# Another order in the first two steps of a Mamba mixer: third projection pair before the cumulation, softplus in two parts

## The reference

```python
h = rmsnorm(layernorm(x), ln1_w)
z, xs, Bs, Cs, dt = split(h @ w_in.T)               # widths 512, 128, 128, 512, 4
xs, Bs, Cs = silu(conv4(concat(xs, Bs, Cs)) + conv_b) # causal, depthwise, 4 taps
dt = softplus(dt + dt_bias)
a = dt * -exp(A_log)
cs = cumsum(a, within each chunk of 128)
att = (Cs @ Bs.T) * exp(cs_q - cs_k)[lower triangle] * dt_k
y = att @ xs + (Cs @ state) * exp(cs) + D * xs      # state carried from chunk 0 to chunk 1
out = (y * silu(z)) @ w_out.T
```

## Time and profile before

| What | Value |
|---|---|
| median of 3 runs | 1748.95 us (1748.63 to 1749.5) |
| profiled execution, its own time | 1752.33 us |
| its span | 1750.6 us |
| PE busy | 1644.1 us, 94% |
| DVE busy | 1084.1 us, 62% |
| ACT busy | 792.1 us, 45% |
| POOL busy | 604.3 us, 35% |
| mean granted clock of PE | 0.986 of full speed |

### The profile page before, as it was taken

The page is one execution under the profiler, slowest core; times in us unless marked ns, Lnnn a source line. Parts: engine busy times, 40 slices in busy tenths (PEclk is TensorE's granted clock), DMA queues, the critical chain, the costliest instruction groups (busy, mean ns, idle before and its releaser), DMA issues. The chain is left out here.

```text
span 1750.6 us, 26151 instructions
## 1 busy us (share of the span) xinstructions
PE 1644.1 (94%) x8965; PEld 1378.9 (79%) x8965; DVE 1084.1 (62%) x2298; ACT 792.1 (45%) x1723; POOL 604.3 (35%) x792
## 2 busy tenths in 40 slices
PE   4999999999999999999999999988999999999984
PEld 4898987888888888777877888767888888888873
DVE  6888876525565554574334233556777877877773
ACT  3676664223223232222222222217877777776860
POOL 4455463211111111432111111465354444444422
PEclk8999999999999999999999999999999999999997
DMA  4000011000111101421011011210000000000000
GB/s 138 21 17 21 1 37 53 25 25 22 30 28 42 35 17 35 130 71 57 16 34 38 28 37 48 73 37 13 1 7 7 13 1 14 13 1 13 14 7 19
DMA packets 32967, 54.26 MB, mean 31 GB/s; under 512 B 3840, under 2 KB 9120, under 8 KB 32832
## 3 DMA queue, kind: packets, MB, share of 16 engines
q1 hardware_dynamic: 32832, 52.55, 9.8%
HBM read 43.10 MB, written 9.44 MB: 30 GB/s over the span
## 5 line engine op out<-in xcount | busy, mean ns | idle before, releaser
L1280 POOL TENSOR_TENSOR m_a_lo<-m_prod,m_a_hi 128x512 fp32r<-128x512 f32 x100 | 134.8, 1348 | 635.4 <-ACT m_a_hi L1362 635.4
L1515 DVE TENSOR_TENSOR m_prod<-m_prod,a_ps 128x512 f32<-128x512 f32 x100 | 68.8, 688 | 386.4 <-ACT m_prod L1356 386.4
L1356 ACT ACTIVATE m_prod<-a_ps 128x512 f32<-128x512 f32 x100 | 59.8, 598 | 546.3 <-PE a_ps L128 546.3
L2074 ACT ACTIVATE t_p<-a_ps,t_nmax 128x128 f32<-128x128 f32 (+1 forms) x512 | 182.9, 440 | 4.7 <-DVE t_nmax L2171 3.8
L2177 DVE TENSOR_TENSOR t_pT_lo<-a_ps,t_pT_hi 128x512 fp32r<-128x512 f32 x192 | 132.5, 690 | 73.5 <-ACT t_pT_hi L2067 72.6
L2171 DVE TENSOR_REDUCE t_nmax<-a_ps 128x2 f32<-128x512 f32 (+1 forms) x192 | 131.1, 683 | 24.9 <-PE a_ps L2249 18.1
L2067 ACT ACTIVATE t_pT_hi<-a_ps 128x512 fp32r<-128x512 f32 x192 | 118.6, 618 | 61.4 <-PE a_ps L2260 60.6
L128 PE MATMUL a_ps<-m_hT_hi,m_w_lo 128*128 128x512 f32 x312 | 123.9, 397 | 0.0
L126 PE MATMUL a_ps<-m_hT_hi,m_w_hi 128*128 128x512 f32 x312 | 123.1, 395 | 0.4 <-DVE f_w_lo L1420 0.4
L127 PE MATMUL a_ps<-m_hT_lo,m_w_hi 128*128 128x512 f32 x312 | 123.3, 395 | 0.0
L2260 PE MATMUL a_ps<-consts,t_p 128*128 128x128 f32 x768 | 115.8, 273 | 0.8 <-ACT t_p L2074 0.6
(11 more groups left out here) (287 smaller groups left out, 4677.6 us busy)
## 6 DMA issues: line engine op xcount, KB each, us to landing
m_raw<-in_w_mlp SPq DMA_DIRECT2D x75, 256.0 KB, 2.7
a_xt<-in_x SPq DMA_DIRECT2D x8, 512.0 KB, 3.7
t_yl<-in_x SPq DMA_DIRECT2D x16, 256.0 KB, 4.2
x_store<-stream SPq DMA_DIRECT2D x4, 1024.0 KB, 5.1
t_yl<-x_store SPq DMA_DIRECT2D x16, 256.0 KB, 2.7
out<-t_yl SPq DMA_DIRECT2D x16, 256.0 KB, 2.0
a_raw_y<-in_w_mixer SPq DMA_DIRECT2D x10, 256.0 KB, 4.1
m_raw<-in_w_attn SPq DMA_DIRECT2D x10, 256.0 KB, 2.8
```

What stands on the lines that cost most here:

```text
L1280: pool.tensor_tensor(a_lo[:, n % 2, :], prod[:, :], f(a_hi[:, n % 2, :]), ALU.subtract).then_inc(lo, 1)
L1515: dve.tensor_tensor(prod[:, :], prod[:, :], ps[:, U + TURN_AT["unit", n, 0] % 2, :], ALU.mult).then_inc(prodd, 1)
L2074: last = act.activation(p[:, u % 2, h * width:(h + 1) * width], unit_bank(u)[:, h * width:(h + 1) * width], ACT.Exp, bias=nmax[:, u % 3, h ...
```

## The change

In turn -1, PE runs the third projection pair of sequence 0 before the cumulation, not behind it; the transposes of the cumulated values (`cs_turned(0)`) move from in front of `h_turned(1)` to behind the fifth pair. DVE's part of the softplus is cut in two, `softplus_mid` and `softplus_end`; for sequence 0, the first runs before the first convolution and the second behind it. DVE normalises sequence 1 before it goes on with weight tiles 4 to 7 and the softplus, and ACT's Exp and Ln for sequence 0 come behind the first tap. Tiles 6 and 7 are split in turn -2. Of tiles 8 to 11, two stand between the first and second convolution and two behind the statistics; ACT writes the high halves of 10 to 13 behind the first silu of Cs. POOL scales five tiles, not four, before the second `norm_roots`. `misc_turns` is the table that tells which PSUM bank a short-lived result takes and what must have been read there before; it follows the new order, so that `h_turned(1)` waits no longer for `cs_out(0)`.

```diff
@@ misc_turns
+        if b == -1:
+            turns = ("h0", b + 2), ("h1", b + 2), ("csT", b + 1), ("xk", b + 1)
@@ gpsimd_program
-        for n in range(4):
+        for n in range(5):
             scale_weight(n)
         norm_roots(1)
-        for n in range(4, SCALED):
+        for n in range(5, SCALED):
@@ scalar_program
-            if b == -1:
-                weight_high(6)
-                weight_high(7)
             if there(f_):
                 tapped(f_, 0)
             if b == -1:
-                for n in range(8, 12):
-                    weight_high(n)
+                softplus(0)
+                weight_high(8)
+                weight_high(9)
...
-            if there(f_):
+            if there(f_) and f_:
                 cs_out(f_)
...
             if b == -1:
-                weight_high(12)
-                weight_high(13)
+                for n in range(SCALED, NW):
+                    weight_high(n)
             if there(g):
                 steps_out(g)
             if b == -2:
-                weight_high(4)
-                weight_high(5)
+                for n in range(4, 8):
+                    weight_high(n)
...
                 silu_z(f_, 4)
+                if f_ == 0:
+                    cs_out(0)
                 kx_high_(f_)
...
-            if there(g):
+            if there(g) and g:
                 softplus(g)
@@ vector_program
-            if b == -1:
-                weight_low(6)
-                weight_low(7)
...
                 convolve(f_, 0)
             if b == -1:
-                for n in range(8, 12):
-                    weight_low(n)
-            if there(f_):
+                softplus_end(0)
+                weight_low(8)
+                weight_low(9)
+            if there(f_) and f_:
                 cumulated(f_)
...
             if b == -1:
                 statistics(e)
+                weight_low(10)
+                weight_low(11)
+                cumulated(0)
...
                 weight_low(3)
-                softplus_in(0)
-                weight_low(4)
-                weight_low(5)
-                softplus_out(0)
...
                 normalise_again(e)
+            if b == -2:
+                weight_low(4)
+                weight_low(5)
+                softplus_in(0)
+                weight_low(6)
+                weight_low(7)
+                softplus_mid(0)
@@ tensor_program
-            wait(pe, csv_done, g - 1)
+            wait(pe, csv_done, g - 1 if g > 1 else g)
...
                 project(0, 1)
-                cumulate(0)
...
                 project(f_, 2)
             if f_ == 0:
-                cs_turned(0)
+                cumulate(0)
...
                 project(f_, 4)
+                if f_ == 0:
+                    cs_turned(0)
```

More of the change, by code:

```diff
@@ L149, in misc_turns @@
     for b in range(FIRST_STEP, BATCH):
-        for what, batch in (("csT", b + 1), ("state", b), ("h0", b + 2), ("h1", b + 2), ("xk", b + 1), ("out0", b), ("out1", b)):
+        turns = ("csT", b + 1), ("state", b), ("h0", b + 2), ("h1", b + 2), ("xk", b + 1), ("out0", b), ("out1", b)
+        if b == -1:
+            turns = ("h0", b + 2), ("h1", b + 2), ("csT", b + 1), ("xk", b + 1)
+        for what, batch in turns:
             if 0 <= batch < BATCH:
@@ L615, in softplus_in, with softplus_mid @@
             dve.scalar_tensor_tensor(S(1), S(0), -1.0, S(0), ALU.mult, ALU.min).then_inc(sp_step, 1)
-        def softplus_out(g):
+        def softplus_mid(g):
             S = lambda k: sp_t[:, g % 2, k, :]
@@ L625, in softplus_out, with softplus_end @@
             dve.scalar_tensor_tensor(S(2), S(6), -1.0, S(5), ALU.mult, ALU.mult).then_inc(sp_step, 1)
+        def softplus_end(g):
+            S = lambda k: sp_t[:, g % 2, k, :]
             dve.wait_ge(sp_step, 7 * g + 6)
@@ L790, in vector_program @@
             if there(g) and g:
-                softplus_out(g)
+                softplus_mid(g)
+                softplus_end(g)
             if there(f_):
```

## The result

The changed kernel took 1753.47 us (median of 20 runs, 1748.86 to 1759.43), the kernel before 1748.84 us beside it (20 runs, 1747.8 to 1752.58). The ratio is 1.002, with a 95% interval of 1.0011 to 1.0028. It is slower, by 4.6 us by the medians: clear of noise, though only 0.2 to 0.3% of the whole. Its runs also lie much farther apart. The forecast was 1748.5 with a range to 1750.6: wrong.

What follows compares the result with a forecast made beforehand. PE, busy 94% of the span, was taken as the bound, through its waits and clock. Terms: -2.1 us for the fifth pair, +0.4 tail, +1.3 clock, so -0.4 us: 1748.5 us, range 1745.2 to 1750.6.

Steps and rivals of the forecast that it cites:

- The clock in the second gap: PE's wait for L607 ahead of the dt product: 2.6 us long, clock more likely than not falls, costing 1.3 us (0.5 to 2.3).
- the first gap: PE's wait for the first convolution ahead of the third pair: convolution at 29.25, PE restarts at 31.73, 2.90 us earlier.
- the new wait: DVE's tiles 10 and 11 wait for ACT's high halves, over 3 us, ahead of L607; third convolution still 2.1 us earlier.
- The slower rival: Clock stays low from the second gap through dt product, fifth pair and next pair: 6.0 us lost, 1753.2 us; chance 0.04.
- The premise under that price: From the old trace: clock falls some 2.3 us after PE stops and returns about 6 us after it restarts.
- my lower bound of 2.0: First convolution's least gain, 2.0 us earlier, if POOL hinders both tiles by 0.92 us.
- The third pair: PE's projection pair behind the first gap: still at low clock, 5.29 us, ending at 37.02.
- The tail: Moved `cs_turned(0)` and ACT's copy behind the fifth pair make everything up to sequence 1's cumulation 0.4 us later (0 to 0.8).
- Without the clock: Sum before pricing low clock in the second gap: -2.1 + 0.4 = -1.7 us.
- Passing it on one to one: What is gained before about 58 us reaches the total time whole, as PE is fully busy from 130 to 200 us.
- the signs of being wrong that I named: PE restarting before 30 us, third pair at full clock, or cumulation of sequence 1 at 54 us or earlier.

Runs made afterwards that it cites:

- both traces of the changed kernel: Changed kernel, no edit: first trace from the 20-run result, 1753.47 us; second from repeating it against the kernel before, 1753.38 us, ratio 1.0035.
- The second trace of before: The kernel before, unedited, run again beside itself: 1748.51 us, ratio 0.9998.
- The fillers: Idle 128x512 matmuls in both gaps: changed kernel with 19 and 11, 1746.41 us; kernel before with 19 and 5, 1746.51 us.

## Why the prediction was wrong

- **The clock in the second gap** is the step that failed. I put the fall there as likelier than not, which both traces of the changed kernel show, but priced it at 1.3 us, 2.3 at most, because before the clock had come back about 6 us after PE's restart. It measured 4.0 us in the median. In the first trace, the fastest of 20, the clock was back about 3.4 us after the restart at 45.82; only the dt product was slow (3.19 us from its start to the transposes, 2.01 before), and the price was 1.2 us. In the second it was low until some 9 us after the restart at 45.87: the dt product and the whole fifth pair ran at 1.2 GHz (5.3 us instead of 2.85), and the price was 3.6 us. PE's work and its pause for ACT's copy were the same in both, so they don't explain the difference; what does is open. In the first trace the terms add up: the fifth pair, foreseen at 46.4, began at 49.28, later by 1.3 us for the first gap, 0.4 for the new wait and 1.2 for the clock. The slower rival had the mechanism in part: the low clock went through the fifth pair in one of two traces, but not through the next one. I gave it 0.04, and its price of 6.0 us for the clock was nearer to 4.0 than the forecast's 1.3.
- **The premise under that price** was one trace. I took the return of the clock 6 us after a restart, and its fall 2.3 us into a gap, as if they repeat. The second trace of before has the return about 3 us after the restart. Behind PE's last matmul ahead of the first gap, the clock fell after about 4.2 us in the first trace of the changed kernel and about 2.2 us in the second. With tiles 10 and 11 moved, it didn't fall in that gap at all, but behind it.
- **The first gap** is a second term that was mis-sized: foreseen 2.90 us earlier, found 1.57. Foreseen were the convolution at 29.25 and the third pair at 31.73; found 30.58 and 33.06. The normalisation beside the scaling took 4.74 us (foreseen 4.90). I missed two terms. L715 was blocked by POOL's fifth tile, 0.85 us, on the path to every later instruction of DVE; I took the end of POOL's roots, 19.99, over from the old trace, as if the tile moved ahead of them held up nothing. It was 20.88. And tiles 4 and 5 took 2.98 us, not 2.21, for they met both POOL's last tile and the skip matrix; with the skip matrix elsewhere they took 2.13. The two aren't independent: without POOL's fifth tile the third pair came only 0.1 us earlier. The 1.57 us lie outside even my lower bound of 2.0, which had no room for L715.
- **The new wait.** Its mechanism was right, and its size nearly: DVE waited 3.82 us ahead of tile 10, I had written over 3. L610 started 6.14 us after the third pair's end, foreseen 5.7; the pair of splits took 2.17 us beside POOL's low half of Cs instead of 1.29, 0.88 more, where I took 0.4. By the rule of the Trainium skill that the prediction cites ("SBUF — State Buffer", section "Who interferes with whom") the term would have been up to 0.9, and this trace agrees with it. But I only booked the wait as a part of a gain, and did not see that it was the part to object to. Without it the kernel is 7.4 us faster.
- **The third pair** at the low clock took 5.29 us in the first trace, foreseen 5.29; 5.13 in the second. **The tail**: from the fifth pair's end to the cumulation 6.43 us, 6.01 before, so 0.42; foreseen 0.4. Moving it back gave 0.54.
- **Without the clock** I had -1.7 us. The fillers give -0.1 by the medians and -0.6 by the traces. The shortfall is about the 1.3 us of the first gap.
- **Passing it on one to one** isn't borne out. From the cumulation to the end the traces took 1693.2 and 1690.4 us before, 1688.5 and 1688.6 in the changed kernel, 1690.4 in both kernels with fillers, 1691.5 with tiles 10 and 11 moved. These differences are as large as the effect that I forecast; the medians over many runs are needed. By luck, the traced execution of the changed kernel took 1748.86 us, next to the forecast of 1748.5, though its cumulation stood 1.16 us behind that of before.
- **The range** was too narrow: the cases of a low clock are not a term with a mean but a spread of about 10 us, which the 20 runs show. None of the signs of being wrong that I named came; I had named none for a kernel that is slower.

Open: the longest executions, up to 1759.43 us. By span times clock all of their loss is low clock, to about 0.9 us, but none of them was traced, and I can't say whether it all lies in the first 60 us. Two of 27 runs of the kernel before in one comparison took 1755.64 and 1755.78 us, and five of 33 in another between 1753.06 and 1755.67; they are as unexplained.

## What to carry to other kernels

Before filling an engine's idle time with work, look at what that work itself waits for: a weight tile that hangs on another engine's queue turned idle time of DVE into a later start of what PE needed. Here a gap of PE of two or three us had to be priced at its length plus the slow stretch behind it, and that second part varied from run to run. Closing the gap helped most (7.4 us), and throwaway matmuls that ended before the gap did helped too (4.0 us). One trace isn't enough to price such a stretch: take a second one of the kernel before. And an engine that is idle isn't free to use: ask which instructions of another engine it will hold up.

## What was unexpected of the hardware

- The stretch at low clock behind a gap of similar length was not fixed. Behind the second gap of the same program, with the same instructions at the same times to 0.1 us, it ended before 50 us in one execution and near 55 us in another.
- Nor did the length of a gap alone decide where the clock fell: it fell inside gaps of 3.15 and 3.59 us, but a gap of 4.24 us was passed at 1.00, with the fall about a us behind it, and it fell behind one of 2.27 us as well.
- A VectorE instruction of 16 elements a partition took 1.01 us instead of 0.16, beside a GpSimd one of 1.22 us.
- 19 idle matmuls of 128x512 (4.6 us) in a gap of 5.2 us made the program faster by 3.0 us (1749.4 to 1746.4).
